# The last expert stage of a graph network on one core: ranks, expert, sum and store in one stage

## The reference, cut to what matters

```
xn   = layernorm(x)                       # 3125 x 256
w    = xn @ wr + br                       # one score for each node
pick = w is among the 1561 largest        # ties go to the lower node number
y    = gelu_tanh(xn @ w1 + b1) @ w2 + b2  # 256 -> 1024 -> 256
x    = x + xn + where(pick, w * y, 0)     # the block's own residual, and the layer's
```

## Time and profile before

| what | value |
|---|---|
| median of three runs | 7236.09 us |
| the profiled execution's own time | 7226.2 us |
| its span (first to last instruction) | 7224.5 us |
| PE busy | 5231.8 us (72%) |
| DVE busy | 4189.8 us (58%) |
| ACT busy | 2279.4 us (32%) |
| mean granted TensorE clock | 0.869 |

### The profile page before, as it was taken

The page is one execution under the profiler, slowest core; times in us unless marked ns, Lnnn a source line. Parts: engine busy times, 40 slices in busy tenths (PEclk is TensorE's granted clock), DMA queues, the critical chain, the costliest instruction groups (busy, mean ns, idle before and its releaser), DMA issues. The chain is left out here.

```text
span 7224.5 us, 76506 instructions
## 1 busy us (share of the span) xinstructions
PE 5231.8 (72%) x21589; PEld 3552.3 (49%) x21589; DVE 4189.8 (58%) x6678; ACT 2279.4 (32%) x4039; POOL 1424.1 (20%) x1466
## 2 busy tenths in 40 slices
PE   0222778879788779989869769849946777667976
PEld 0000344444444456668757547738833333336754
DVE  6200389974899832232278354211139999997857
ACT  0000211112111123322256213312226777765621
POOL 0677066640566500001100000020020000000000
PEclk9755888989899879999989889879978888888988
DMA  1111433345333510003342002245634444433200
GB/s 27 27 37 36 190 106 101 111 88 228 124 107 106 97 26 9 17 2 113 111 127 94 13 12 59 92 127 183 183 104 147 155 154 156 151 109 116 84 13 18
DMA packets 379948, 679.56 MB, mean 94 GB/s; under 512 B 94754, under 2 KB 306907, under 8 KB 372156
## 3 DMA queue, kind: packets, MB, share of 16 engines
q1 hardware_dynamic: 304364, 519.11, 22.0%
q0 software_dynamic: 75344, 157.40, 8.3%
HBM read 503.61 MB, written 172.62 MB: 94 GB/s over the span
## 5 line engine op out<-in xcount | busy, mean ns | idle before, releaser
L605 POOL DMA_INDIRECT sum_rows_in<-rel_table,rel_row x880 | 843.3, 958 | 444.9 <-issue 235.7
L629 DVE TENSOR_SCALAR sum_hot_cell<-x_nodes 128x1500 bf16<-128x1500 f16 (+1 forms) x880 | 892.2, 1014 | 1.8 <-issue 1.8
L683 PE MATMUL ps<-sum_hot_cell,sum_hot_src 128*128 128x500 bf16 x2640 | 771.8, 398 | 150.6 <-issue 85.1
L1793 PE MATMUL ps<-att_ring,acc 125*65 125x500 f32 x1000 | 601.8, 688 | 307.1 <-DVE att_ring L1615 307.0
L552 PE MATMUL ps<-rel_diag,rel_xt 128*128 128x512 f32 x800 | 436.4, 694 | 406.8 <-ACT rel_stage L511 179.4
L688 PE MATMUL ps<-sum_rows_in,sum_hot 128*128 128x256 f32 x1760 | 596.9, 419 | 62.2 <-issue 58.6
L1801 PE MATMUL ps<-acc,att_ring 125*125 125x257 f32 x2500 | 565.3, 389 | 73.8 <-DVE att_ring L1615 46.4
L1731 ACT ACTIVATE att_ring<-att_ring,att_src 125x625 f32<-125x625 f32 x750 | 545.5, 804 | 125.2 <-DVE att_ring L1596 125.2
L1596 DVE TENSOR_TENSOR att_ring<-att_ring,att_rows 125x3125 f32<-125x3125 f32 (+1 forms) x162 | 512.6, 3170 | 95.3 <-ACT att_ring L1690 94.7
L1690 ACT ACTIVATE att_ring<-att_rows,att_src 125x625 f32<-125x625 f32 x750 | 547.7, 804 | 31.9 <-PE ps L1801 30.9
L1801 PEld LDWEIGHTS ps<-acc,att_ring 125*125 125x125 f32 x2500 | 478.6, 192 | 157.8 <-DVE att_ring L1615 59.4
(11 more groups left out here) (434 smaller groups left out, 7911.9 us busy)
## 6 DMA issues: line engine op xcount, KB each, us to landing
att_cell<-cells SPq DMA_DIRECT2D x150, 781.2 KB, 4.7
att_masks<-masks SPq DMA_DIRECT2D x150, 762.9 KB
rel_table<-rel_stage SPq DMA_DIRECT2D x50, 2048.0 KB, 6.3
ffn_w<-in_L_ffn_W SPq DMA_DIRECT2D x64, 1024.0 KB, 7.1
sum_cell<-cells SPq DMA_DIRECT2D x125, 156.2 KB, 5.5
sage_cell<-cells SPq DMA_DIRECT2D x125, 156.2 KB, 2.2
masks<-sum_stage POOLq DMA_DIRECT2D x25, 762.9 KB, 11.9
sum_rows_in<-rel_table,rel_row POOLq DMA_INDIRECT x880
```

The lines of the kernel that those rows point to most:

```text
L605: pool.indirect_dma_start(rows_in[:, b, u, :], None, table, bass.IndirectOffsetOnAxis(rows[:, k:k + 1], 0)).then_inc(gathered[b], 16)
L629: dve.tensor_scalar(hot_cell[:, b, u, :], K.columns[:, :, 0:CW], K.cell[:, k], None, ALU.is_equal).then_inc(s_hot, 1)
L683: pe.matmul(K.ps[:, bass.ds(side * 4 + j, 1), 0:BW].rearrange("p a n -> p (a n)"), hot_src[:, b, u, :], hot_cell[:, b, u, j * BW:(j + 1) * ...
L1793: pe.matmul(K.ps[0:W, side, 0:BAND], node_rows[s][0:NPT, h, :], ring[0:NPT, b % RB, v, 0:BAND], start=s == 0, stop=s == NT - 1).then_inc(s ...
```

## The change

`TokenWeights.batch` gets five additions, x plus xn, one for each tile of the batch. The phases pick, ffn3, res4 and store become one phase, `last_expert`. Its loops are written out, so that all waits are for constants. The results go to four banks, DVE lags with the sums by four tiles behind the ranks, multiplies by the gate and adds in one operation, and SP stores five tiles at a time.

```diff
@@ TokenWeights.batch
         dve.tensor_tensor(self.K.token_w[:, i * UN:(i + 1) * UN], ps[:, :, 0],
                           tools.vec[self.bias_name][:, :].to_broadcast([P, UN]), ALU.add)
+        for t in range(i * UN, (i + 1) * UN):
+            dve.tensor_tensor(self.K.x[:, t, :], self.K.x[:, t, :], self.K.aux[:, t, :], ALU.add)
@@ in place of rank_rows, node_ranks, add_largest, store
+def last_expert(K, tag, load, act, count, out):
+    OUT, LATE = 4, 4
...
+        def ps_one(q):
+            return K.ps[:, q % 4, 0:HF]
+        def ps_out(t):
+            return K.ps[:, 4 + t % OUT, 0:D]
+        def ps_row(i):
+            a, b = cuts[i]
+            return K.ps[:, 6 + i % 2, 0:b - a]
+        @block.sync
+        def _(sp):
...
+                load(sp, 0, 0, w1[:, :, :], w2[:, :, :], b1[:, :], b2[:, :], w_in)
+            rows = out.rearrange("(t p) d -> p t d", p=NPT)
+            for i in range(NCH):
+                tiles = slice(i * UN, (i + 1) * UN)
+                sp.wait_ge(s_final, (i + 1) * UN)
+                sp.dma_start(rows[0:112, tiles, :], K.x[0:112, tiles, :]).then_inc(stored, 16)
+                sp.dma_start(rows[112:NPT, tiles, :], K.x[112:NPT, tiles, :]).then_inc(stored, 16)
...
+        @block.vector
...
+            dve.wait_ge(w_in, 64)
+            def rank_of(t):
+                if t > 0:
+                    dve.wait_ge(s_rank, t)
+                dve.scalar_tensor_tensor(out=found[:, :], in0=all_rows[:, :], scalar=own[:, t:t + 1],
+                                         in1=earlier[:, N - t * NPT:2 * N - t * NPT], op0=ALU.is_equal, op1=ALU.mult).then_inc(s_equal, 1)
+                dve.wait_ge(s_equal, t + 1)
+                dve.scalar_tensor_tensor(out=found[:, :], in0=all_rows[:, :], scalar=own[:, t:t + 1], in1=found[:, :],
+                                         op0=ALU.is_gt, op1=ALU.add, accum_out=rank[:, t:t + 1]).then_inc(s_rank, 1)
+            def add_row(t):
+                dve.wait_ge(s_rank, t + 1)
+                dve.scalar_tensor_tensor(out=gate[:, t:t + 1], in0=rank[:, t:t + 1], scalar=float(count), in1=K.token_w[:, t:t + 1],
+                                         op0=ALU.is_lt, op1=ALU.mult).then_inc(s_gate, 1)
+                dve.wait_ge(s_out, t + 1)
+                dve.tensor_tensor(K.acc[:, t, 0:D], ps_out(t), b2[:, :], ALU.add).then_inc(s_y, 1)
+                dve.wait_ge(s_gate, t + 1)
+                dve.wait_ge(s_y, t + 1)
+                dve.scalar_tensor_tensor(out=K.x[:, t, :], in0=K.acc[:, t, 0:D], scalar=gate[:, t:t + 1], in1=K.x[:, t, :],
+                                         op0=ALU.mult, op1=ALU.add).then_inc(s_final, 1)
+            for t in range(NT + LATE):
+                if t < NT:
+                    rank_of(t)
+                if t >= LATE:
+                    add_row(t - LATE)
...
+        @block.tensor
...
+                if i >= 2:
+                    pe.wait_ge(s_copied, i - 1)
+                pe.matmul(ps_row(i), K.ones[:, :], flat_diag[:, a:b], start=True, stop=True).then_inc(s_row, 1)
+            pe.wait_ge(s_copied, len(cuts))
+            pe.wait_ge(w_in, 64)
+            for ch in range(NCH):
...
+                for u in range(UN):
+                    t = ch * UN + u
+                    if t >= OUT:
+                        pe.wait_ge(s_y, t - OUT + 1)
...
```

More of the change, by code:

```diff
@@ L2441, in node_ranks @@
[L2441 to L2449, removed]
@@ L2452, in add_largest @@
[L2452 to L2464, removed]
-                                          op0=ALU.is_lt, op1=ALU.mult))
-            link(dve.tensor_tensor(y, y, gate[:, :].unsqueeze(2).to_broadcast([P, NT, D]), ALU.mult))
-            link(dve.tensor_tensor(K.x[:, :, :], K.x[:, :, :], K.aux[:, :, :], ALU.add))
-            dve.tensor_tensor(K.x[:, :, :], K.x[:, :, :], y, ALU.add)
@@ L2524, in store @@
-def store(K, out):
-    nc = K.nc
-    with Phase(nc, "store") as ph:
-        stored = ph.sem("stored")
-        block = ph.block()
-        @block.sync
-        def _(sp):
-            rows = out.rearrange("(t p) d -> p t d", p=NPT)
-            sp.dma_start(rows[0:112], K.x[0:112, :, :]).then_inc(stored, 16)
-            sp.dma_start(rows[112:NPT], K.x[112:NPT, :, :]).then_inc(stored, 16)
-            sp.wait_ge(stored, 32)
+                if i >= 2:
+                    pe.wait_ge(s_copied, i - 1)
@@ new lines, in _ @@
+                pe.matmul(ps_row(i), K.ones[:, :], flat_diag[:, a:b], start=True, stop=True).then_inc(s_row, 1)
+            pe.wait_ge(s_copied, len(cuts))
+            pe.wait_ge(w_in, 64)
+            for ch in range(NCH):
+                for q in range(QS):
+                    hc, half = q // 2, q % 2
+                    n = ch * QS + q
+                    if n >= 4:
+                        pe.wait_ge(s_h, n - 3)
+                    for c in range(DC):
+                        mm = pe.matmul(ps_one(q), w1[:, c, hc * P:(hc + 1) * P],
+                                       K.xt[:, c, ch * CH + half * HF:ch * CH + (half + 1) * HF], start=c == 0, stop=c == DC - 1)
+                    mm.then_inc(s_one, 1)
+                pe.wait_ge(s_h, (ch + 1) * QS)
+                for u in range(UN):
+                    t = ch * UN + u
+                    if t >= OUT:
+                        pe.wait_ge(s_y, t - OUT + 1)
+                    for hc in range(HC):
+                        mm = pe.matmul(ps_out(t), h[:, hc, u * P:(u + 1) * P], w2[:, hc, :], start=hc == 0, stop=hc == HC - 1)
+                    mm.then_inc(s_out, 1)
@@ L2709, in build @@
                   keep_xt=True, keep_xn=True, gates=TokenWeights(K, "L3_ffn_br"), cols=1)
-        with ExitStack() as scope:
-            def scoped(name, shape, dt=F32):
-                return scope.enter_context(nc.sbuf_tensor(name, shape, dt))
-            K.rank_rows, K.earlier = scoped("rank_rows", [P, N])[:, :], scoped("earlier", [P, 2 * N], BF16)
-            K.found, K.own_value = scoped("found", [P, N], BF16), scoped("own_value", [P, NT])
-            K.rank = scoped("rank", [P, NT])
-            rank_rows(K, "pick")
-            wide_experts(K, "ffn3", 1, 1, 8, ACT.Gelu_apprx_tanh, load_only, K.acc[:, :, 0:D], beside=node_ranks(K))
-            add_largest(K, "res4", N // 2 - 1)
-        store(K, out)
+        last_expert(K, "ffn3", load_only, ACT.Gelu_apprx_tanh, N // 2 - 1, out)
 def kernel(**inputs):
```

112 lines of the change are left out of this document (45 added, 67 removed).

## The result

The changed kernel takes **7162.68 us** (median of 4 runs, 7160.97 to 7164.85), the kernel before 7233.7 us (4 runs, 7229.92 to 7247.7). The ratio is 0.9898, with a 95% interval of 0.9881 to 0.9916: 1.0% faster. The forecast was 7162 us, with a range of 7143 to 7188.

What follows compares the result with a forecast made beforehand. DVE's three operations over all tiles were taken as the bound. Terms +1.7 - 10.5 - 33.3 - 21.8 - 10.1 = -74.0 us, against the median 7236.09, gave 7162 us, range 7143 to 7188.

Steps and rivals of the forecast that it cites:

- five pieces: Last scores to span's end: ranks' front part, weights' wait, expert 233.0 us, gate and three operations 21.8, store 15.15.
- one gap: DVE's turn in the expert's stage: dependent operations follow after 0.04 us, as in written-out code, giving 7.91 a turn.
- the gaps stay: Rival for DVE's turn: the loop's gaps remain, 8.3 us a turn instead of 7.91; 7173 us, chance 0.17.
- Weights: Before DVE's first rank: loading issued at the phase's start removes the wait and phase boundary, -10.5 us.
- Additions: In prep3: 25 additions, 1.7 us a batch, four batches hidden behind PE; +1.7 us, range 1.7 to 8.5.
- Four banks: Expert's stage: no DVE wait for PE except before the last tile; stage 233.0 to 199.7 us, -33.3.
- is wanted a full lag later: At chunk borders: a chunk's first result needs at most 27.8 us and is wanted after 38.7, four turns plus 7.05.
- The end of the stage: Last tile: its result waits for tile 20's bank; its sum starts 4.5 to 6.2 us after tile 20's, taken as 5.4.
- The store: After DVE's end: only the last fifth remains, 5.0 us instead of 15.15, including 0.5 for clearing 15 semaphores; -10.1.
- the prediction's second source: For the last store: a transfer takes about 2.0 us plus bytes at 436 GB/s, 3.5 us against 4.4 from rows.
- Slower: Rival: PE bounds the stage at the lower clock, chunk 71 us; gain gone from 54; 7314 us, chance 0.03.

Runs made afterwards that it cites:

- the second set: The unchanged changed kernel timed again on another chip against the kernel before (7 runs): median 7156.74 us against 7234.76, ratio 0.9888.

## Why the prediction was right

**Which piece ends last.** The working cut the time into five pieces that follow each other, each from rows, and each came out within 1.0 us. This worked because DVE carries the stage and its turn could be put together from durations that the change doesn't touch (3.47, 3.48, 0.42, 0.48) and one gap, taken from the earlier trace rows. That gap was the choice on which 8 us hung; a turn of 7.90 against the forecast 7.91 shows that it was right. The rival "the gaps stay" is out. That the turn fits to 0.01 is in part luck: the sum starts 6.97 us into the turn (7098.74 - 7091.77) where the forecast had 7.05, and the product 0.53 behind the sum's start where it had 0.46, and the two cancel.

**Weights.** The gap of 10.63 us became 0.03. With the load late it is back (+9.1 us). That is 1.4 less than the forecast's 10.5: in that kernel the load is issued 0.03 us behind the own scores (6946.15 against 6946.12) and not 1.1 as in the kernel before, where a phase border lay between, and the transfer took 9.06 and not 9.5.

**Additions.** +1.7, four batches hidden behind PE: the idle times before the scores shrank by as much as the additions take, and leaving them out moves no scores.

**Four banks.** Right in the result (no wait at borders, one at the end), wrong in the reason. The step that failed is "is wanted a full lag later". The slack belongs to the banks, five turns with four of them and three with two. For two banks and a lag of four the step gives no wait, and 4.6 to 4.7 us at a border was measured; for four banks and a lag of one it gives 12.8, and none was measured. That it gave the right answer for this kernel is luck. Two smaller terms of this item were high: ACT's 1.05 us was 0.62, and so PE's chunk 35.6 instead of 36.1.

**The end of the stage.** The sum of tile 24 was forecast 5.4 us behind that of tile 20; it came 5.85 behind (7152.00 - 7146.15), since the last 16 matmuls took 5.35 us after idling, near the upper end of 6.2 that the forecast named. The last product started 0.90 behind its sum's start (7152.90 - 7152.00) instead of 0.46. With the sum of tile 20 at 193.5 us after the first rank, forecast 193.4, this is the 1.0 us by which the stage is over its forecast. What the product waited for was not found; one other, at 7020.26, shows the same.

**The store.** The mis-sized term. From DVE's end to the span's end were 5.9 us, forecast 5.0. The data came as forecast (7157.0, 3.6 us behind DVE's end; forecast 3.6). From the last data to the end it was 2.3 us instead of 0.9 + 0.5. SP's waits at the end of the program, in the changed kernel and in the one before:

```profile
SPq L115 <- DMA out<-x_nodes: 2.9, 1, 2.9
...
SPq L115 <- DMA out<-x_nodes: 8.5, 1, 8.5
```

From the end of its last issue (7154.44 and 7215.24) SP waits this long for the transfers, so 2.0 us are left behind their landing now, and 0.8 before. With all stores at the end it is 2.0 too (7164.21 + 3.4 to 7169.6). So the missing time lies at the end of the phase and not in the store. The phase has 15 semaphores to clear there instead of 1, which the forecast put at 0.5; whether they account for it was not tried.

On the prediction's second source: the section "Anatomy of one DMA" of "DMA: Bandwidth & Descriptors" in the Trainium skill gives its figures for transfers issued from GpSimd, and here SP issues them. Its 3.5 us stand beside 7157.3 - 7153.41 = 3.9 from the first issue to the landing.

**The chances.** "Slower" needed a chunk of over 54 us on PE. Even with all results doubled it was 52.65, and that stretch was still 15 us shorter than before's; by its 4.4 us for each us a chunk the gain would be gone at about 56.

**The time.** The timed gain is 71.0 us by the medians of the first four runs and 78.0 by the second set, around the 73.1 of the stretch. The forecast of 7162 rests also on the median of runs that lie 18 us apart; that it was met within 1 us is in part luck. For the profiled execution the forecast was 7152.2, and it took 7160.97, 8.8 more: 7.9 of them came before prep3, where nothing was changed, and 0.9 in the stretch.

## What to carry to other kernels

Where two engines hold each other up through result buffers, count from the release of a buffer to the use that needs it, in turns of the slower engine: that slack grows with the number of buffers and not with how late the consumer reads. Reading late helps at the start, where the first result has to be made. Cost an operation that is to be put beside others by a row in which it stands beside those others: moving a sum off the busy engine was worth 0.6 us a tile on paper (7.90 to 7.30) and gave back most of it on the engine that took it over. And before comparing two executions, look for the place up to which the kernels are the same, and subtract it.

## What the runs showed of the hardware that was not expected

- A matmul of one row (1x256, fp32, two records) at the end of a group cost 4.27 - 3.52 = 0.75 us, where one of 128 rows, two records as well, costs 3.52 / 8 = 0.44. Few rows did not make it cheap.
- GpSimd's fp32 addition of 128x256 took 0.73 us beside short operations of DVE, mostly with one input, and 2.36 us in the mean beside DVE's passes with two, and made DVE slower as well (turns of up to 8.79 us instead of 7.30).
- Code with constants in its waits starts a dependent pass on DVE 0.03 us behind the one before it, where with registers it was 0.22; behind an accumulator's read the sum starts after 0.04 (6713.09 against 6713.05) instead of 0.42.
- The four chips of the experiments ran the part before prep3 at two paces, 4% apart: 6590.1 to 6610.4 us on two of them, 6881.0 to 6896.7 on the others, with DVE's passes in the stretch behind it alike. Almost all of it lies before 2490 us: the first gather comes at 919.5 us in the kernel before and at 727.7 in the one with written-out loops, the gathers then last until 2487.0 and 2185.0, and from there to prep3 both take about the same (4401 and 4416). The 25 stores of the table ahead of the gathers are issued within 633 us in one and 222 in the other. The cause stays open.
